# Reordering the step of a fused attention kernel: projection and mask last, one product behind the squares

## The reference

```
x = attn_layer(shift_tokens(x)) + x      # window attention, 16 heads of 64, window 32
x = ffn_layer(shift_tokens(x)) + x       # layer norm, gated feed-forward

attn_layer:  q, k, v = split(x @ Wqkv)
             q, k = l2norm(q) * qs, l2norm(k) * ks          # per head
             q = q*cos*scale + rotate_half(q)*sin*scale     # k with 1/scale
             sim = 8 * q k^T over this and the previous window, masked by a band
             out = softmax(sim) v ;  return out @ Wo
```

## Time and profile before

| | |
|---|---|
| median of 3 runs | 4112.42 us (4110.75 to 4112.66) |
| profiled execution | 4110.29 us |
| its span, first to last instruction | 4108.5 us |
| mean granted clock of TensorE | 0.987 |
| full steps with a projection | 384 (6 layers x 8 sequences x 8 steps) |

### The profile page before, as it was taken

The page is one execution under the profiler, slowest core; times in us unless marked ns, Lnnn a source line. Parts: engine busy times, 40 slices in busy tenths (PEclk is TensorE's granted clock), DMA queues, the critical chain, the costliest instruction groups (busy, mean ns, idle before and its releaser), DMA issues.

```text
span 4108.5 us, 187519 instructions
## 1 busy us (share of the span) xinstructions
PE 3858.4 (94%) x79584; PEld 3036.2 (74%) x79584; DVE 3149.0 (77%) x5678; ACT 3145.3 (77%) x10376; POOL 2542.0 (62%) x2584
## 2 busy tenths in 40 slices
PE   6888885999999999989999999999899999999998
PEld 3555554888876888848888668888488886688884
DVE  6878874888866888848888668888488886688884
ACT  5777785888865888848888658888488886588883
POOL 4766675766645666637666456666376664566660
PEclk9999998999999999999999999999999999999999
DMA  1000001111111111111111111111111111111110
GB/s 35 2 2 2 2 2 46 48 50 46 46 62 32 49 47 50 42 50 47 48 47 46 60 36 47 45 50 42 53 45 50 45 47 59 36 47 45 50 42 27
DMA packets 100907, 166.88 MB, mean 41 GB/s; under 512 B 26224, under 2 KB 33648, under 8 KB 99824
## 3 DMA queue, kind: packets, MB, share of 16 engines
q1 hardware_dynamic: 100080, 154.89, 12.8%
HBM read 26.13 MB, written 2.10 MB: 7 GB/s over the span
## 4 chain that ended last, share of the span: by engine, by line
PE 77%; DVE 2%; POOL 1%; issue 1%; ACT 1%; DMA 0%; SPq 0%; DVEq 0%; POOLq 0%; ACTq 0%
PE s_bank L1197 13%; PE s_bank L1268 10%; PE s_bank L1286 10%; PE s_bank L1177 5%; PE s_proj L1220 5%; PE s_proj L1222 4%; PE s_proj L1221 4%; PE s_bank L1159 4%; PE s_bank L1311 3%; PE s_bank L1245 2%; PE s_bank L1247 2%; PE s_bank L1248 2%; PE s_bank L1234 2%; PE s_bank L1233 2%; PE s_bank L1232 2%; PE s_bank L1187 2%
## 5 line engine op out<-in xcount | busy, mean ns | idle before, releaser
L818 POOL TENSOR_TENSOR s_rotated<-s_rotated,s_by_sin 128x512 f32<-128x512 f32 x768 | 978.7, 1295 | 291.3 <-DVE s_by_sin L1106 290.7
L919 ACT ACTIVATE s_probs<-s_bank,s_neg_max 128x64 f32<-128x64 f32 x3072 | 900.3, 309 | 2.8 <-DVE s_neg_max L1042 2.6
L827 POOL TENSOR_TENSOR s_probs<-s_probs,s_rden 128x256 f32<-128x256 f32 x768 | 454.8, 613 | 658.0 <-DVE s_rden L1049 658.0
L1101 DVE TENSOR_TENSOR s_rotated<-s_proj,s_cos 128x1024 f32<-128x1024 f32 x384 | 469.0, 1221 | 258.4 <-ACT s_sq L942 254.9
L919 ACT ACTIVATION_READ_ACCUMULATOR s_probs<-s_bank,s_neg_max 128x1 f32 x3072 | 632.4, 206 | 0.0
L1197 PE MATMUL s_bank<-s_qk 32*32 32x64 f32 x49152 | 598.2, 224 | 8.9 <-issue 8.3
L1197 PEld LDWEIGHTS s_bank<-s_qk 32*32 32x32 f32 x49152 | 530.7, 103 | 94.6 <-issue 93.5
L791 DVE SCALAR_TENSOR_TENSOR s_qk<-s_inv_norm,s_rotated 128x512 f32<-128x512 f32 x768 | 578.5, 793 | 1.4 <-ACT s_inv_norm L969 1.1
L834 POOL TENSOR_TENSOR s_sq<-s_sq 128x512 f32<-128x512 f32 x384 | 490.3, 1277 | 137.2 <-ACT s_sq L942 137.1
L1220 PE MATMUL s_proj<-s_xs_high,s_w_high 128*128 128x256 f32 x1536 | 497.6, 324 | 59.1 <-POOL s_xs_rest L809 31.2
L213 POOL TENSOR_TENSOR s_probs<-s_probs,s_rden 128x384 f32<-128x384 f32 (+3 forms) x512 | 406.4, 802 | 207.2 <-DVE s_rden L406 203.4
(11 more groups left out here) (123 smaller groups left out, 8635.0 us busy)
## 6 DMA issues: line engine op xcount, KB each, us to landing
s_v<-s_v SPq DMA_DIRECT2D x384, 192.0 KB
s_v<-s_v SPq DMA_DIRECT2D x384, 64.0 KB
s_qk<-f_wqk SPq DMA_DIRECT2D x6, 1024.0 KB, 5.4
s_xs_raw<-u SPq DMA_DIRECT2D x48, 128.0 KB, 2.6
s_xf<-u SPq DMA_DIRECT2D x48, 128.0 KB, 2.6
s_xs_raw<-u SPq DMA_DIRECT2D x48, 127.8 KB, 2.7
s_xf<-u SPq DMA_DIRECT2D x48, 127.8 KB, 3.1
s_qk<-f_wv SPq DMA_DIRECT2D x6, 512.0 KB, 6.2
```

What stands on the lines that cost most here:

```text
L818: nc.gpsimd.tensor_tensor(rotated[:, par, :, half, :], rotated[:, par, :, half, :], by_sin[:, :, 1 - half, :], (ALU.subtract, ALU.add)[half])\
L919: last = nc.scalar.activation(probs[:, par, h, b, :], score_bank[h][:, b * KEYS:(b + 1) * KEYS], ACT.Exp, scale=-1.0, bias=neg_max[:, par, ...
L1101: nc.vector.tensor_tensor(rotated[:, par, :, :, :], proj_ps[:, :, :, :], rot_cos[:, :, :, toks], ALU.mult).then_inc(S["prod_done"], 1)
```

## The change

The data and the matmuls stay as they are but for the type of the mask (`ident_b`, `band_b` in bf16 become `ident_r`, `band_r` in F32R, a rounded 32-bit type). The order within a step becomes:

- PE: scores, transposes, norm sum, output projection, values, probabilities times values, (LayerNorm mean in step 5, variance in step 6), projection, and last the mask for the scores of the next step.
- ACT: (log_var in step 7), keys_down, exponentials(0), Ln, (LayerNorm square in step 6), exponentials(1), copy of v, y_high, square, Exp.
- DVE: least(0), copy of probabilities, least(1), the sine product of the unit of the step before, q/k write, the two sums inverted, y_rest of the unit just multiplied, (residual addition in step 4, centre in step 5), cosine product, (divide in step 7, scale_shift in step 0).
- POOL: the squares of queries and of keys added one after the other (two instructions of half the size, each with its own count of `sqadd_done`), rotations one step later than before (LAG_NORM), tokens_rest, normalise.

`sq` and `y_high` now have one buffer instead of two, `by_sin` has two instead of one. The diff is cut to its core (waits and moved bodies that stay the same are left out). The buffers:

```diff
-        sq = sb("s2_sq", [P, 2, 2, 2, TOKS])
-        by_sin = sb("s2_by_sin", [P, 2, 2, TOKS])
+        sq = sb("s2_sq", [P, 2, 2, TOKS])
+        by_sin = sb("s2_by_sin", [P, 2, 2, 2, TOKS])
...
-        y_high = sb("s2_y_high", [P, 2, 2, TOKS], F32R)
+        y_high = sb("s2_y_high", [P, 2, TOKS], F32R)
```

In the step of POOL:

```diff
-                    nc.gpsimd.tensor_tensor(own[:, :, 0, :], own[:, :, 0, :], own[:, :, 1, :], ALU.add)\
-                      .then_inc(S["sqadd_done"], 1)
-                    pool.wait_ge(S["prod_done"], 2 * m + 2)
+                    for i in range(2):
+                        nc.gpsimd.tensor_tensor(sq[:, i, 0, :], sq[:, i, 0, :], sq[:, i, 1, :], ALU.add)\
+                          .then_inc(S["sqadd_done"], 1)
+                if live(s, p, LAG_NORM, first):
+                    pool.wait_ge(S["prod_done"], 2 * (n - LAG_NORM) + 2)
                     rotate(0)
                     rotate(1)
```

In the step of ACT:

```diff
+                if ln and p == LN_STEP + 2:
+                    log_var(f)
                 if live(s, p, LAG_VALUE, first):
                     keys_down()
                 if live(s, p, LAG_SCORE, first):
                     exponentials(0)
+                if live(s, p, LAG_MIX, first):
+                    act.wait_ge(S["ss_done"], m + 1)
...
+                if ln and p == LN_STEP + 1:
+                    centred_square(f)
                 if live(s, p, LAG_SCORE, first):
                     exponentials(1)
...
+                if full:
+                    act.wait_ge(S["proj_done"], n + 1)
+                    if not (first and p == 0):
+                        act.wait_ge(S["ss_done"], n)
+                    nc.scalar.activation(sq[:, :, :, :], proj_ps[:, :, :, :], ACT.Square)\
+                      .then_inc(S["sq_done"], 1)
```

In the step of DVE:

```diff
                 if score:
                     least(0)
-                    least(1)
...
+                if score:
+                    least(1)
+                if live(s, p, LAG_MIX, first):
+                    if not (first and p < LAG_MIX + 2):
+                        dve.wait_ge(S["add_done"], 2 * m - 2)
+                    nc.vector.tensor_tensor(by_sin[:, par, :, :, :], proj_ps[:, :, :, :],
+                                            rot_sin[:, :, :, half * TOKS:(half + 1) * TOKS], ALU.mult)\
+                      .then_inc(S["prod_done"], 1)
...
-                if not first and s > 1 and p == 0:
-                    divide(l, s - 2)
-                    scale_shift(l, s - 2)
...
+                if ln and p == LN_STEP:
+                    centre(l * NSEQ + s - 1)
...
+                if ln and p == LN_STEP + 2:
+                    divide(l, s - 1)
+                if not first and s > 1 and p == 0:
+                    scale_shift(l, s - 2)
```

In the step of PE:

```diff
-                    pe.wait_ge(S["norm_done"], m + 1)
-                    for e in range(2):
-                        nc.tensor.matmul(score_bank[e][:, 0:NW * KEYS], ident_b[:, :], band_b[:, 1 if half or e else 0, :],
...
+                    if full and not first and p == LN_STEP + 1:
+                        pe.wait_ge(S["f_xc"], l * NSEQ + s)
+                    if full and not first and p == LN_STEP + 2:
+                        pe.wait_ge(S["f_log"], l * NSEQ + s)
+                    for i in range(2):
+                        pe.wait_ge(S["sqadd_done"], 2 * m + i + 1)
+                        last = nc.tensor.matmul(ss_bank[:, i * TOKS:(i + 1) * TOKS], same_head[:, :],
+                                                sq[:, i, 0, :], start=True, stop=True)
...
+                if full and not first and p in (LN_STEP, LN_STEP + 1):
+                    pe.wait_ge(S["log_done"], n)
+                    (ffn_mean if p == LN_STEP else ffn_var)(l * NSEQ + s - 1)
...
+                if live(s, p, LAG_SCORE - 1, first):
+                    pe.wait_ge(S["norm_done"], n + 1 - LAG_SCORE + 1)
+                    if not (first and p == LAG_SCORE - 1):
+                        pe.wait_ge(S["exp_done"], 2 * (n + 1 - LAG_SCORE))
+                    for e in range(2):
+                        nc.tensor.matmul(score_bank[e][:, 0:NW * KEYS], ident_r[:, :], band_r[:, 1 if half or e else 0, :],
+                                         start=True, stop=False, skip_group_check=True)
```

More of the change, by code:

```diff
@@ L930, in step @@
                     exponentials(0)
[L931 to L943, removed]
-                    act.wait_ge(S["v_mm"], n + 1)
-                    nc.scalar.activation(v[:, p // TILES, 2 * (p % TILES), :], tr_bank[:, :], ACT.Copy)\
-                      .then_inc(S["v_done"], 1)
[L948 to L953, removed]
-                    nc.scalar.activation(y_high[:, place(p, LAG_VALUE)[2], :, :],
-                                         y_bank[:, :].rearrange("p (a t) -> p a t", a=2), ACT.Copy)\
-                      .then_inc(S["y_done"], 1)
                 if live(s, p, LAG_MIX, first):
@@ L1086, in step @@
                     inverse_sum(1)
+                if live(s, p, LAG_VALUE, first):
+                    m = n - LAG_VALUE
+                    dve.wait_ge(S["y_done"], m + 1)
+                    if not (first and p == LAG_VALUE):
+                        dve.wait_ge(S["wo_done"], m)
+                    nc.vector.tensor_tensor(y_rest[:, :, :], y_bank[:, :].rearrange("p (a t) -> p a t", a=2),
+                                            y_high[:, :, :].bitcast(F32), ALU.subtract).then_inc(S["y_rest"], 1)
                 if not first and p == WO_STEP - 1:
@@ L1235, in step @@
                       .then_inc(S["v_mm"], 1)
-                if live(s, p, LAG_WO, first):
-                    m = n - LAG_WO
-                    quad, half, par = place(p, LAG_WO)
-                    pe.wait_ge(S["y_done"], m + 1)
-                    pe.wait_ge(S["y_rest"], m + 1)
-                    if p == LAG_WO and not first:
-                        pe.wait_ge(S["attn_res"], l * NSEQ + s)
-                    for pair in range(2):
-                        into, w = wo_bank[:, half * TOKS:(half + 1) * TOKS], [part[:, 2 * quad + pair, :] for part in wo]
-                        nc.tensor.matmul(into, w[0], y_high[:, par, pair, :], start=(p == LAG_WO and pair == 0),
-                                         stop=False, skip_group_check=True)
-                        nc.tensor.matmul(into, w[0], y_rest[:, pair, :], start=False, stop=False, skip_group_check=True)
-                        last = nc.tensor.matmul(into, w[1], y_high[:, par, pair, :], start=False,
-                                                stop=(quad == QUADS - 1 and pair == 1), skip_group_check=True)
-                    last.then_inc(S["wo_done"], 1)
                 if live(s, p, LAG_VALUE, first):
@@ new lines, in step @@
+                if full:
+                    if not (first and p == 0):
+                        pe.wait_ge(S["prod_done"], 2 * n)
+                    quad, half, _ = place(p, 0)
+                    at = WIN + half * TOKS
+                    for i in range(2):
+                        for c in range(2):
+                            w = [part[:, quad, 2 * i + c, :] for part in wqk]
+                            nc.tensor.matmul(proj_ps[:, i, c, :], w[0], xs_high[:, s % 2, at:at + TOKS], start=True, stop=False)
+                            nc.tensor.matmul(proj_ps[:, i, c, :], w[0], xs_rest[:, s % 2, at:at + TOKS], start=False, stop=False)
+                            last = nc.tensor.matmul(proj_ps[:, i, c, :], w[1], xs_high[:, s % 2, at:at + TOKS],
+                                                    start=False, stop=True)
+                    last.then_inc(S["proj_done"], 1)
```

103 lines of the change are left out of this document (47 added, 56 removed).

## The result

The changed kernel takes 4198.94 us (median of 4 runs, 4193.76 to 4205.7), the kernel before, run beside it, 4111.59 (median of 4): ratio 1.0219, interval [1.0203, 1.0236]. That is 87 us slower where 22 were forecast, and above the range.

The account below looks back on a forecast made before the run. TensorE, without a gap in the plain step (7.27 us in either order), was taken to bound the kernel. Terms 4 + 10 + 9 + 5 + 11 - 20 + 3 = +22 us gave 4133 us, range 4080 to 4180.

Parts of the forecast that it names:

- (c): Step 7: norm sum waits for f_log, the log of the variance, starting at 2.2 instead of 1.95; +10 us.
- (d): Step 0: divide, now ahead of DVE's first minimum, waits out the second addition and delays values; +9 us.
- (e): Step 1: scale_shift, last in step 0, stands before the minimum, making it 0.47 late, 0.15 on PE; +5 us.
- (f): Step 3: tokens_rest runs right behind the second rotation, so the q/k write and mask start late; +11 us.
- (a): PE's mask: weight load grows from 98 to some 190 ns, mostly hidden, 0.01 us each step; +4 us.
- Rival 1: Divide loses its turn to the first rotation, so the minimum starts 1.8 late; +43, 4176 us; chance 0.15.
- (b): PE: entering a 128-wide matmul from small tiles costs 0.10 us, now paid by projection, not norm sum; zero.
- (g): LayerNorm's mean moves from step 6 to the end of step 5; zero, at worst 13 us.
- rival 4: The rounded mask's weight loads are exposed on PE; +71 us on 4133, 4204; chance 0.06.
- Rival 3: No change to be measured: PE's bound rules, run-out and new waits cancel; 4112 us; chance 0.15.
- Rival 2: Faster: late starts of (c) to (f) vanish, the run-out's y_rest waits fall away in full; 4083 us; chance 0.22.

Follow-up runs that it names:

- all edits made: Changed kernel with norm sum behind output projection, divide and scale_shift ahead of cosine product, tokens_rest last, bf16 mask, run-in reordered: 4089.83 us, ratio 0.9949.

## Why the prediction was wrong

The forecast's terms beside what the experiments measured. The two sides each sum to their total; the last row is what remains of the changed kernel's order with all edits made (4089.8 less 4109.1), so it is not measured by itself. The measured column goes by edit, in the order in which they were made, and an edit also moves time in stages that its row doesn't name; by stage the traces have +91 for the steps, +18 for the run-in, -20 for run-out and feed-forward, +4 from there to the next layer's scores and +3 ahead of the first scores of all.

| | forecast | measured |
|---|---|---|
| plain steps and (c), (d), (e) | 0 + 10 + 9 + 5 = 24 | 80.5 |
| (f) tokens_rest | 11 | 11.4 |
| run-in (steps 1 and 2 reordered) | 3 | 13.6 |
| (a) mask | 4 | 3.6 (10 as long as the run-in's spells hang on it) |
| run-out and all else | -20 | -19 |
| sum | +22 | +90 |

**The step that failed** is the sentence "GpSimd (POOL) adds the squares in two halves of 0.64 (half of 1.27), done at 1.6 and 2.2 of the next step; norm sum wants them at 1.95 and 2.4. Hidden, 0.1 to spare." Both sides of it were off. The addition of half the columns lasts 0.73, not 0.64, and the square's end reaches GpSimd 0.08 later: the second was done at 2.39 behind the scores (1944.74 less 1942.35) where I had 2.2. And the second half wants it not when its matmul should start but at its weight load, 0.32 before the load in fact began, at 2.12. The margin of 0.2 (my two times for the second half; the sentence says 0.1) was a deficit of 0.3. Of this, 0.21 us shows against the same kernel with the norm sum moved (7.41 for 7.20) and 0.14 against the kernel before (7.27); that the matmuls of the first half cover the rest is a guess. Moving the norm sum won 35 us alone, moving divide 38, both together 80.5 of the 87. The last sentence of the prediction had a loop through square, cosine product and copy as its danger; the loop was the other branch behind the same square. With 0.1 to spare in a sum of six durations, the plain step deserved a rival of its own: a tenth of a microsecond there is 38 us, more than any term that I added, and yet it had no chance of its own. The trace before even held the rows to size it: in stage 1 GpSimd multiplies 512 columns in 1.125 us and 256 in 0.709 (L213), and L827's 256 take 0.613: half the columns never cost half.

**(d)** had the mechanism right: divide starts behind the cosine product while the second addition runs, gets in ahead of the rotation, and holds up the minimum. The size was wrong. It lasts 0.87 (I named 0.7 to 0.8), where the kernel before has 0.68 for it undisturbed and I had reckoned with 0.55. The minimum started 0.8 late (2.87 for 2.06 behind the scores), not 0.6; the 0.2 more are the second addition's, which ends at 2.4 and not at 2.2, so the mis-sized addition is in this term too. And values followed the copy's end (2055.58) by 0.26, not 0.1: the 0.26 became 0.67 in step 0. With (e), 0.23 in step 1 against 0.15, the two are worth 38 us where I had 14 (28 in the 56 steps, most of the rest in the third row of the table of stages, where I had nothing). **Rival 1**, by which divide loses its turn, did not come: that would have been over 1.2.

**(c)** was right in place: step 7 takes 0.14 more than a plain one, and it went with the loop's cure. The profile names no releaser for most of these weight loads, but in the step seen (2046.20) the load starts 0.07 us after the log of the variance ends. **(f)** was right in kind: step 3 takes 0.42 more than a plain one, of which step 4 regains 0.14. But I multiplied by 36 and left out step 3 of each layer's first sequence, where the wait is 1.68 us: of the 15 us that its edit won in steps and run-ins by the traces, half lay there. That the medians give 11.4 where I had 11 is luck. **(b) and (g)** cost nothing that shows: plain steps of 7.19 with the norm sum moved leave no room for them. **(a)** holds as well: the weight load grew to 0.188 us as forecast, and the eight steps sum to the same with either mask, so rival 4 is refuted, though its number, 4204, was the nearest to the result. That is why a time that fits is no proof of a cause.

**The run-in** was the second thing missed. I let values be exposed and gave 0.5 us a layer, 3 in all; it grew by 18. The largest part with a name is the wait for the q/k write in step 3 of the first sequence, 1.3 us more a layer than before, which is term (f) in a place where I hadn't counted it. Behind it, step 4 takes 8.0 to 8.1 us in five layers and 6.7 in the first; in all five the windows there show the clock lowered. Ahead of the first scores, the norm sum, moved ahead of both value projection and projection, has nothing before it in steps 1 and 2 and waits 1.9 and 2.0 us; the kernel before waited there too, for the sine product, so that stretch grew by only 4 us in five layers. Covering 0.7 of each wait won 13.6, more than these 4: it shortened not only these waits but step 3 behind them (6.5 to 5.7 us, mean of six layers).

**The run-out** was right, in kind and in size: y_rest's waits gone, waits for the q/k write and the probabilities in their place, 3.3 us less a layer up to the end of the feed-forward where I had 3 to 4, -20 in all as forecast; the three new waits are 1.5, 1.1 and 1.9 us, where my times gave 1.6, 1.0 and 1.9. Rival 3, that all cancels, is out by the interval. Rival 2's gain was there, and the early y_rest alone makes 26 us without the rest of the change.

## What to carry to other kernels

When a chain of four engines is to close within a step, its slack must be reckoned at the last wait that is issued (a weight load goes ahead of its matmul) and with instruction lengths from rows of that very size; if the slack is less than the sum of the guesses in it, the loop is a rival, multiplied by the number of steps. Move the one instruction that PE waits for, and look at the steps that have no cover (the first ones of a run-in) as closely as at the steady one: count a delay in every step where its instruction stands. Of a reorder with many parts, try each part alone: here one moved instruction gained as much as all parts together after four corrections (0.9938 and 0.9949, intervals that overlap).

## What the runs showed of the hardware

- GpSimd's tensor_tensor on f32 takes 0.730 us for 128x256 and 1.274 for 128x512: 2.1 ns for each column and some 0.19 for each instruction (1.274 less 512 x 2.125; 544 columns, at 1.35, fit). The rate agrees with the Trainium skill ("GPSIMD Engine Reference", section Elementwise — side-by-side cycle accounting), which has 2048 columns in 4.497 us, 2.2 ns each; it names the dispatch of an instruction as a cost, without a figure for GpSimd. With one operand broadcast, 256 columns take 0.613.
- How long PE rests does not by itself decide whether the clock falls. Behind the same wait of 1.92 us it fell in the third layer of the changed kernel (0.50 above) and stayed up in the second (norm sum from 1298.61 on, first lines below); behind the same 1.68 us it fell with the rounded mask and stayed up with the bf16 one. It stayed up behind 1.22 and 1.32, and also in the kernel before behind 2.89 us (PE empty from 1843.33 to 1846.22, last lines):

```profile
1298.10:1300.10 2.00, 1.49 (x6) 1.01 (x7) 2.00 (x2) 0.07 (x1) 1.14 (x2) 1.00 0.82 242
1300.10:1302.10 2.00, 2.00 (x15) 1.71 (x13) 0.12 (x1) 1.22 (x2) 0.00 (x0) 1.00 0.22 47
```

```profile
1844.00:1846.00 2.00, 0.00 (x0) 0.00 (x0) 2.00 (x2) 0.20 (x1) 1.05 (x1) 1.00 0.76 250
1846.00:1848.00 2.00, 1.78 (x14) 1.74 (x15) 0.16 (x1) 0.06 (x1) 1.76 (x2) 1.00 0.74 186
```

- The same run-in takes two lengths, 36.6 or 38.1 us, by one spell more or less in step 4; with divide late, the layers of one execution are split between them. What tips a layer stays open, and with it why the bf16 mask was at the shorter in all layers. The rounded mask in the kernel before was not tried.
